# First stage of a bitonic level reads its pair from PSUM, or changes the sign itself

## What is computed

```python
xn = layernorm(x)                            # x (6250, 256)
# two layers: mean over a node's neighbours, then a product, a norm, silu
for W, b, g, beta in layers:
    agg = segment_sum(h[dst], src, num_segments=6250) / degree
    h = silu(norm((h + agg) @ W.T + b) * g + beta)
# a linear attention over all rows
q, k, v = split(xn @ w_qkv.T)                # 8 heads of 64
mix = q @ (instance_norm(k).T @ instance_norm(v)) / N @ w_out.T + b_out
x = x + h + mix
x = x + moe_ffn(layernorm(x))                # two experts of eight, 512 wide, gelu, layer norm
```

## Time and profile before

| | us |
|---|---|
| median of three runs | 3220.04 |
| lowest and highest | 3218.69 and 3220.16 |
| the profiled execution's own time | 3224.08 |
| its span (first to last instruction) | 3222.3 |
| DVE busy in the span | 2000.9 |
| PE busy in the span | 2600.2 |
| mean granted TensorE clock | 0.927 |

### The profile page before, as it was taken

The page is one execution under the profiler, slowest core; times in us unless marked ns, Lnnn a source line. Parts: engine busy times, 40 slices in busy tenths (PEclk is TensorE's granted clock), DMA queues, the critical chain, the costliest instruction groups (busy, mean ns, idle before and its releaser), DMA issues. The chain is left out here.

```text
span 3222.3 us, 54447 instructions
## 1 busy us (share of the span) xinstructions
PE 2600.2 (81%) x16782; PEld 1835.7 (57%) x16782; DVE 2000.9 (62%) x4822; ACT 1306.1 (41%) x2213; POOL 170.0 (5%) x160
## 2 busy tenths in 40 slices
PE   0776455575868888887679999999899999976997
PEld 0343333342335445443348888888688888864665
DVE  8998999899989889899912222222122222246555
ACT  0443222265647677666832222222122222235666
POOL 0000000000000000000000000000011111124000
PEclk9988778797989999999979999999899999988999
DMA  5000000024213233233334444444544444411000
GB/s 164 0 1 0 1 0 0 11 81 158 85 72 128 97 118 131 87 128 114 115 120 142 145 152 142 146 151 136 192 136 139 133 137 136 136 38 37 20 26 28
DMA packets 153846, 304.75 MB, mean 95 GB/s; under 512 B 28963, under 2 KB 125476, under 8 KB 153700
## 3 DMA queue, kind: packets, MB, share of 16 engines
q1 hardware_dynamic: 101796, 217.44, 21.4%
q10 hardware_dynamic: 51776, 85.24, 7.3%
q0 software_dynamic: 128, 0.26, 0.0%
HBM read 196.54 MB, written 106.37 MB: 94 GB/s over the span
## 5 line engine op out<-in xcount | busy, mean ns | idle before, releaser
L1088 PE MATMUL banks<-outer,ring 128*128 128x257 f16 x2450 | 544.0, 274 | 15.4 <-DMA outer<-table,heavy 8.4
L1088 PE MATMUL banks<-tabs,ring 128*128 128x257 f16 x2450 | 542.3, 274 | 8.5 <-DMA ring<-counts 8.5
L1089 PE MATMUL banks<-outer,ring 128*128 128x256 f16 x2450 | 543.8, 273 | 0.0
L1089 PE MATMUL banks<-tabs,ring 128*128 128x256 f16 x2450 | 542.2, 273 | 0.0
L744 ACT ACTIVATE ring<-banks 128x512 f16<-128x512 f32 x637 | 382.5, 600 | 378.1 <-POOLq L605 376.2
L1057 PE MATMUL banks<-ring 128*128 128x512 f16 x1102 | 340.3, 421 | 135.6 <-SPq L504 60.9
L745 ACT ACTIVATE banks<-banks 128x512 f32<-128x512 f32 x637 | 384.1, 603 | 0.0
L1664 DVE TENSOR_SCALAR ring<-val,outer 128x512 f16<-128x512 f16 x1102 | 316.0, 345 | 21.5 <-PE banks L1057 21.4
L1057 PEld LDWEIGHTS banks<-ring 128*128 128x128 f16 x1102 | 153.1, 147 | 295.8 <-issue 255.3
L1088 PEld LDWEIGHTS banks<-outer,ring 128*128 128x128 f16 x2450 | 238.7, 97 | 48.8 <-DMA outer<-table,heavy 8.6
L1057 PE MATMUL banks<-outer,ring 128*128 128x512 f16 x549 | 195.6, 423 | 84.2 <-DVE big L1664 50.5
(11 more groups left out here) (340 smaller groups left out, 3442.6 us busy)
## 6 DMA issues: line engine op xcount, KB each, us to landing
ring<-counts SPq DMA_DIRECT2D x98, 800.0 KB, 4.7
counts<-ring ACTq DMA_DIRECT2D x84, 896.0 KB, 3.9
ring<-counts SPq DMA_DIRECT2D x98, 768.0 KB, 4.1
tabs<-in_fw SPq DMA_DIRECT2D x4, 2048.0 KB, 9.8
outer<-in_x SPq DMA_DIRECT2D x5, 1280.0 KB, 13.4
outer<-in_x SPq DMA_DIRECT2D x25, 256.0 KB, 2.8
residual<-outer SPq DMA_DIRECT2D x25, 256.0 KB, 2.2
table<-tabs SPq DMA_DIRECT2D x25, 256.0 KB, 2.5
```

The costliest lines, as they stand in the source:

```text
L1088: mm(o[:, 0:D + 1], a, xtab[l][:, cb, D:2 * D + 1], start=cb == 0, stop=False)
L1089: m = mm(o[:, 0:D], a, xtab[l][:, cb, 0:D], start=False, stop=cb == NT - 1)
```

## The change

1. Row part. In levels k = 2 to 10 the first stage is a new `signed_stage(j)`, j = k - 1. It reads keys that have not been negated, and negates the turned one of each pair as it compares: four DVE instructions of 512 keys each, `(turned * -1) min plain` and `(turned * -1) max plain`, for each of the two pairs of a block of four. The nine separate sign changes at line 1371 are gone. The one after level 10, and levels 1 and 11, stay.
2. Even rounds. ACT copies (negating) only the turned half of the keys, as two instructions of 512, one for each half of the columns. DVE copies nothing: its first stage, four instructions of 512, reads the turned key from SBUF and the plain key from PSUM. It writes to `sort[cur]`, the buffer that PE transposed from. The other n // 2 stages follow as before.
3. Odd rounds. ACT copies the first 1024 columns as before. DVE's first stage, distance 1024, two instructions of 1024, reads ACT's copy from SBUF and the other 1024 columns from PSUM. The other ten stages follow as before.
4. The counts of `s_evict`, and which buffer holds the keys at the start of a round (`home`), follow from this.

```diff
+        def signed(cols, d, r):
+            a = cols.rearrange("p (n u d) -> p n u d", u=r // d, d=d)
+            if r == 2 * d:
+                return a[:, :, 1:2], a[:, :, 0:1]
+            return a[:, :, 1:3], a[:, :, 0:4:3]
+
+        def lower_upper(cols, d):
+            a = cols.rearrange("p (n t d) -> p n t d", t=2, d=d)
+            return a[:, :, 0], a[:, :, 1]
...
@@ ACT, rounds
-                act.wait_ge(s_turned, 2 * n + 1)
                 if n % 2 == 0:
-                    (turned, plain), (turned_ps, plain_ps) = flipped(to[:, 0:1024], n // 2), flipped(ps[:, 0:1024], n // 2)
-                    act.activation(turned, turned_ps, ACT.Copy, scale=-1.0)
-                    for o, i in zip(plain, plain_ps):
-                        ins = act.activation(o, i, ACT.Copy)
+                    d, r = 1 << n // 2, min(4 << n // 2, P)
+                    for h in range(2):
+                        half = slice(h * W // 2, (h + 1) * W // 2)
+                        act.wait_ge(s_turned, 2 * n + 1 + h)
+                        act.activation(signed(to[:, half], d, r)[0], signed(ps[:, half], d, r)[0], ACT.Copy, scale=-1.0).then_inc(s_evict, 1)
                 else:
-                    ins = act.activation(to[:, 0:1024], ps[:, 0:1024], ACT.Copy)
-                ins.then_inc(s_evict, 1)
+                    act.wait_ge(s_turned, 2 * n + 1)
+                    act.activation(to[:, 0:W // 2], ps[:, 0:W // 2], ACT.Copy).then_inc(s_evict, 1)
...
@@ DVE
+            def signed_stage(j):
+                nonlocal cur
+                d, r = 1 << j, 4 << j
+                (turned, plain), (low, high) = signed(sort[cur], d, r), [v.rearrange("p (n u) d -> p n u d", u=2) for v in lower_upper(sort[1 - cur], d)]
+                for u in range(2):
+                    dve.scalar_tensor_tensor(low[:, :, u], turned[:, :, u], -1.0, plain[:, :, u], op0=ALU.mult, op1=ALU.min)
+                    ins = dve.scalar_tensor_tensor(high[:, :, u], turned[:, :, u], -1.0, plain[:, :, u], op0=ALU.mult, op1=ALU.max)
+                cur = 1 - cur
+                return ins
...
-                    ins = stage_of(j)
+                    ins = signed_stage(j) if j == k - 1 and 1 < k < LG_W else stage_of(j)
...
-                if k < LG_W - 1:
-                    part = sort[cur].rearrange("p (n r) -> p n r", r=4 << k)[:, :, 1 << k:3 << k]
-                    link(dve.tensor_scalar(part, part, -1.0, None, op0=ALU.mult))
...
-                dve.wait_ge(s_turned, 2 * n + 2)
+                o = sort[cur]
                 if n % 2 == 0:
-                    dve.tensor_scalar(turned, turned_ps, -1.0, None, op0=ALU.mult)
-                    for o, i in zip(plain, plain_ps):
-                        ins = dve.tensor_copy(o, i)
-                    stages = range(n // 2, -1, -1)
+                    stages = range(n // 2 - 1, -1, -1)
+                    for h in range(2):
+                        half = slice(h * W // 2, (h + 1) * W // 2)
+                        dve.wait_ge(s_turned, 2 * n + 2)
+                        dve.wait_ge(s_evict, n // 2 * 3 + 1 + h)
+                        turned, plain = signed(to[:, half], d, r)[0], signed(ps[:, half], d, r)[1]
+                        low, high = [v.rearrange("p (n u) d -> p n u d", u=r // d // 2) for v in lower_upper(o[:, half], d)]
+                        dve.tensor_tensor(low, turned, plain, op=ALU.min)
+                        ins = dve.tensor_tensor(high, turned, plain, op=ALU.max)
                 else:
-                    ins = dve.tensor_copy(to[:, 1024:], ps[:, 1024:2048])
-                    stages = range(LG_W - 1, -1, -1)
-                link(ins)
-                dve.wait_ge(s_evict, n + 1)
-                cur = 1 - cur
+                    stages = range(LG_W - 2, -1, -1)
+                    dve.wait_ge(s_evict, n // 2 * 3 + 3)
+                    dve.wait_ge(s_turned, 2 * n + 2)
+                    dve.tensor_tensor(o[:, 0:W // 2], to[:, 0:W // 2], ps[:, W // 2:W], op=ALU.min)
+                    ins = dve.tensor_tensor(o[:, W // 2:W], to[:, 0:W // 2], ps[:, W // 2:W], op=ALU.max)
+                if len(stages):
+                    link(ins)
```

More of the change, by code:

```diff
@@ L414, in gps_layer @@
         for n in range(ROUNDS):
[L415 to L423, removed]
+            home.append((home[n] + (LG_W - 1 if n % 2 else n // 2)) % 2)
+        def signed(cols, d, r):
[6 more added lines that the diff above has]
+            return a[:, :, 0], a[:, :, 1]
         @block.sync
@@ L956, in _ @@
             pe.wait_ge(s_upto, 1)
-            pe.wait_ge(s_evict, ROUNDS)
+            pe.wait_ge(s_evict, ROUNDS // 2 * 3)
             for k in range(CH):
@@ L1368, in _ @@
                         beside_rows(tick)
-                if k < LG_W - 1:
-                    part = sort[cur].rearrange("p (n r) -> p n r", r=4 << k)[:, :, 1 << k:3 << k]
-                    link(dve.tensor_scalar(part, part, -1.0, None, op0=ALU.mult))
-                elif k == LG_W - 1:
+                if k == LG_W - 1:
                     for h in range(2):
@@ L1385, in _ @@
                     kv_norms(ROW_WINDOWS + n - 1)
-                dve.wait_ge(s_turned, 2 * n + 2)
+                o = sort[cur]
                 if n % 2 == 0:
-                    (turned, plain), (turned_ps, plain_ps) = flipped(to[:, 1024:], n // 2), flipped(ps[:, 1024:2048], n // 2)
-                    dve.tensor_scalar(turned, turned_ps, -1.0, None, op0=ALU.mult)
-                    for o, i in zip(plain, plain_ps):
-                        ins = dve.tensor_copy(o, i)
-                    stages = range(n // 2, -1, -1)
-                else:
-                    ins = dve.tensor_copy(to[:, 1024:], ps[:, 1024:2048])
-                    stages = range(LG_W - 1, -1, -1)
-                link(ins)
-                dve.wait_ge(s_evict, n + 1)
-                cur = 1 - cur
+                    stages = range(n // 2 - 1, -1, -1)
+                    d, r = 1 << n // 2, min(4 << n // 2, P)
+                    for h in range(2):
[6 more added lines that the diff above has]
+                        ins = dve.tensor_tensor(high, turned, plain, op=ALU.max)
+                else:
+                    stages = range(LG_W - 2, -1, -1)
[5 more added lines that the diff above has]
+                    link(ins)
                 for j in stages:
```

## The result

| | before | after |
|---|---|---|
| median, us | 3220.10 (4 runs, 3218.69 to 3220.72) | 3198.33 (4 runs, 3194.39 to 3199.92) |
| ratio | | 0.9932, 95% interval 0.9917 to 0.9947 |
| profiled execution's own time / span | 3224.08 / 3222.3 | 3197.08 / 3195.3 |
| first key instruction to first field of the sorted keys, on DVE | 580.22 | 555.78 |

The change makes the kernel 21.8 us faster by the medians; the interval is 17 to 27 us. The forecast was 3197.

What follows compares the result with a forecast made beforehand. DVE's own instructions, plus a few waits for transposes, were taken to bound the sort. Row part 5.4, odd rounds 8.8, even rounds 2 to 12 7.5 and round 0 1.6 sum to 23.3 us: 3220.0 to 3197, 80% range 3191 to 3206.

Steps and rivals of the forecast that it cites:

- key runs of eight bytes at steps of 32: Row part, level 2's first stage: taken at full rate; half rate would cost 2.1 us once.
- rival 1: Row part: the negating instruction runs at half rate, 19 us lost, gain 4 us, time 3216; chance 0.05.
- round 0: First even round: plain keys in PSUM read at full rate, 1.6 us gained; at the slow rate 0.2.
- The cover: Work beside DVE in the row part and rounds: x's DMAs, PE and ACT keep up, costed at nothing.
- rival 2: Odd rounds: ACT's copy becomes the wait; with all 8.8 us lost, 3205 to 3206; chance 0.04.
- the windows of k and v: Row part, 84 to 255 us: PE and ACT keep up with the shorter DVE work, costed at nothing.
- rival 4: Windows of k and v: the row part's gain returns as waits in `kv_norms`, 5.4 us at most, 3202; chance 0.05.
- Rival 3: Steps, 600 to 1640 us: the gain is lost to PE's clock, slower than before, time 3227; chance 0.03.

Runs made afterwards that it cites:

- e1: Kernel before with the row part alone: nine signed first stages in place of nine sign changes, rounds as before; 3218.88 us, ratio 0.9986.
- e2: Kernel before with the odd rounds alone: DVE's copy gone, first stage reads PSUM; 3212.02 us, ratio 0.9968.
- e3: Kernel before with the even rounds alone: ACT copies the turned keys, DVE's first stage reads the plain ones from PSUM; 3208.13 us, ratio 0.9963.
- e4: Kernel before with round 0's plain keys copied by one instruction of 512 instead of two of 256, on both engines; 3220.81 us in one execution.
- e8: Changed kernel with ACT's copy in odd rounds started only after all sixteen blocks are transposed, not after eight; 3203.41 us, ratio 0.9943.
- e6: Changed kernel with four matmuls of zeros on PE ahead of its wait for sorted rows in rounds 5, 7 and 9; 3195.53 us, ratio 0.9925.

## Why the prediction was right

**The sum.** It had 23.3 us of DVE's instructions; the own time of the sort fell by 23.3 us (567.8 to 544.5). Row part 5.4 foretold, 5.3 in e1; odd rounds 8.8 foretold, 8.6 in e2; even rounds 9.1 foretold, 8.9 in e3. Each price held: 2.53 us for a first stage of four, 1.25 for the copy that went, the same duration with an operand in PSUM. The 2.53 was read in level 2 itself, so the key runs of eight bytes at steps of 32, of which no row had told, cost nothing more. The forecast left the waits as they were. That they came out 1 us smaller in all was not foreseen, and in e2, where PE was slow in every odd round, the waits for keys were 1.5 us longer: in the total of one execution this is luck either way.

**Two unknown costs.** The negating instruction on f32 ran at 684 to 687 ns for 512, so rival 1 fell, and with it the rule of the Trainium skill ("Vector Engine (DVE) Microarchitecture Reference", "Points that are easy to get wrong") that two sources in SBUF that are not bf16 halve such an instruction: 36 instructions here disagree, if half is meant of the plain min or max of the same size, which takes 688 ns. Keys in PSUM at steps of 12 and 4 bytes ran at full rate, so round 0 gave what I took; e4 shows the step of 16 bytes by itself. The PSUM lines of 8 bytes that the Trainium skill gives ("SBUF — State Buffer", section "Door 1: The DMA port swizzle"), where it speaks of matmuls, and which the prediction carried over to DVE's reads, do not explain e4's reads by DVE and ACT: each key is on another such line in both forms, and only one form took 0.34 us more.

**The cover.** Two statements were true only in part. I had ACT's copy end before PE's last block in every odd round, from margins of 0.3 to 0.7 us. These margins hold while PE takes 2.8 us or more for its transposes, as in the odd rounds of the trace before; in rounds 1 and 3 after, PE took 1.97 us, and ACT's copy came last (rival 2 in small): the first stage started 0.2 us after PE's last block. It cost nothing against before, because a wait of 2.2 us replaces one of 3.8 or 2.9. e8 shows what it would cost if ACT were late everywhere: some 5 us of waits, and not the 8.8 of rival 2. And I had the windows of k and v at nothing, from an idle time of 0.04 us an instruction. That average hid the wait of 0.4 us for ACT's squares that the trace before has in the first window. This wait is 0.8 to 2.3 us in the nine executions with the signed row part (0.8, 1.4 and 1.1 in the changed kernel) and 0.2 to 0.9 in the four without it, so rival 4 took about 1 us of its possible 5.4.

**Behind the sort.** Rival 3, a loss in the steps, did not come: from the first field to the last step 1046.1 us after and 1048.3 before, both inside the 1045.5 to 1049.4 of the table's executions. The order of the work there is the same, and the distance does not follow the change. What made it vary by 4 us was not tried. The prediction looked for such a spread in the steps alone; the stretch behind the last step varies by 5.6 us over the same executions, and that it was within 0.2 us in the two compared is chance.

Taken together: 23.3 of own time, 1.1 more because the waits were shorter (12.4 to 11.3), most of it in rounds 1 and 3, where PE's transposes were faster in that execution than in the one of before, 24.4 in the sort; 2.2 in the steps, within their spread from execution to execution; 0.2 behind them; and 0.1 ahead of the sort. That is the 27.0 us between the two spans. By the medians it is 21.8.

## What to carry to other kernels

A copy out of PSUM that is followed by an operation on two tensors can be left out on the slower side: let the operation read one operand from PSUM and the other from a copy made by another engine, and check that this copy ends before the last block arrives. Here its price was nothing up to there, and 0.9 to 1.5 us for a copy of 1.03 behind it. A sign change or a scale that a later two-operand instruction can take in costs only the extra instructions into which the access pattern forces it, 0.13 us a stage here against 0.73. And where runs scatter by as much as the gain, measure the distance between two fixed instructions in the trace, less its waits: it repeated to 0.3 us in three executions of the changed kernel, while the totals of fourteen repeated to 8.5.

## What the runs showed of the hardware

- 512 single f32 keys, read in two series at steps of 16 bytes in PSUM, cost DVE 0.40 us more than one series at steps of 12 and 4 bytes in turn (1.12 against 0.72), of which the second instruction is 0.06, and ACT's took 0.48 us more (1.09 against 0.61) (e4).
- PE's sixteen transposes of f32 blocks took from 1.91 to 3.68 us in the same place of the program: round 7 took 3.67, 1.97 and 3.68 in three executions of the changed kernel, with 4.2, 1.3 and 4.2 us of idle time ahead, and 1.91 in e6, with none. In the odd rounds 1 to 9 much of that time is DVE's wait, and so a part of what the executions differ by.
- DVE's instructions of 512 f32 keys that wait for nothing start 0.60 us apart, though each is recorded with 0.68 or 0.69.
